# A two-layer decoder's last phase: heads' operands ordered by dimension, and a sync queue gated by the softmax maxima's DMA

## The reference

```
q, k = layernorm over the 8 elements of a head, of x @ Wq.T and x @ Wk.T, times g, plus b
v = x @ Wv.T                                   # 16 heads of 8 elements
x = x + softmax(causal(q @ k.T)) @ v @ Wo.T + bo          # self attention

q = layernorm(x) in 16 heads of 8, k = v = context        # no projections
x = x + softmax(window(q @ k.T / sqrt(8))) @ v @ W_proj.T + b   # |i - j| <= 64

x = x + quantise(layernorm(x)) @ quantised weight.T + bias
```

## Time and profile before

| | |
|---|---|
| median of three runs | 1515.22 us (1513.2 to 1517.85) |
| the profiled execution | 1517.21 us, its span 1514.8 us |
| busy share of the span | PE 87%, DVE 72%, ACT 67%, POOL 42% |
| mean granted TensorE clock | 0.924 of full |
| DMA queue of the sync engine (q1) | 85440 packets, 82.35 MB |
| DMA queue of ScalarE (q10) | 1856 packets, 0.79 MB |

### The profile page before, as it was taken

One profiled execution on the slowest core, in us unless ns is written; L12 is line 12 of the kernel. 1 busy time (PEld: TensorE's weight loads), 2 busy tenths in 40 slices (PEclk: granted clock), 3 DMA queues, 4 the chain that ended last, 5 costly groups with the idle time before them and its releaser, 6 DMA issues.

```text
span 1514.8 us, 42023 instructions
## 1 busy us (share of the span) xinstructions
PE 1325.3 (87%) x14969; PEld 952.1 (63%) x14969; DVE 1089.1 (72%) x2570; ACT 1008.9 (67%) x2781; POOL 632.6 (42%) x842
## 2 busy tenths in 40 slices
PE   4358999999999999999849998888988989888885
PEld 1125666766676666676739997555665656665664
DVE  6998889999999888776663444566765767566664
ACT  2129999999999999999925664354544554545552
POOL 0012324443435243202045452376656564644653
PEclk9999999999999999999969999597878898889995
DMA  6952132424223321020123322223012021110100
GB/s 143 244 126 58 46 75 57 111 52 112 58 72 76 83 56 41 16 78 16 36 86 95 92 80 62 82 37 49 16 39 43 26 44 32 24 37 23 32 18 14
DMA packets 91593, 94.21 MB, mean 62 GB/s; under 512 B 17792, under 2 KB 78848, under 8 KB 86912
## 3 DMA queue, kind: packets, MB, share of 16 engines
q1 hardware_dynamic: 85440, 82.35, 22.5%
q0 software_dynamic: 4096, 8.40, 2.0%
q10 hardware_dynamic: 1856, 0.79, 0.2%
HBM read 64.76 MB, written 17.83 MB: 55 GB/s over the span
## 4 chain that ended last, share of the span: by engine, by line
PE 60%; DVE 14%; ACT 9%; issue 8%; DMA 5%; POOL 3%; SPq 1%; another core or an unknown queue 0%; ACTq 0%; DVEq 0%; POOLq 0%
PE P L794 7%; PE P L956 6%; PE P L2129 6%; PE P L1598 4%; PE P L1631 4%; PE P L812 3%; PE P L938 3%; ACT pr L1017 3%; PE P L915 3%; PE P L2192 3%; PE P L2147 3%; DVE mx L2409 3%; PE P L910 3%; PE P L926 3%; PE P L833 2%
## 5 line engine op out<-in xcount | busy, mean ns | idle before, releaser
L2409 DVE TENSOR_REDUCE mx<-P 128x8 f32<-128x1024 f32 x128 | 156.6, 1224 | 169.7 <-PE P L2129 102.3
L2321 ACT ACTIVATE et<-P 128x1024 f32<-128x1024 f32 x128 | 131.1, 1024 | 191.6 <-PE P L2136 182.8
L1017 ACT ACTIVATE pr<-P,nm 128x256 f32<-128x256 f32 x512 | 238.6, 500 | 5.6 <-DVE nm L1218 5.5
L1218 DVE TENSOR_REDUCE nm<-P 128x4 f32<-128x1024 f32 x128 | 156.2, 1220 | 25.6 <-PE P L794 23.3
L794 PE MATMUL P<-kt_w,qt 64*128 64x256 f32 x1024 | 145.2, 402 | 4.6 <-ACT pr L1017 4.6
L999 ACT COPY ptS<-P 128x512 f32<-128x512 f32 x256 | 138.1, 598 | 8.7 <-PE P L812 8.0
L990 ACT ACTIVATE pr<-pr,ri 128x256 f32<-128x256 f32 x254 | 119.6, 536 | 24.6 <-DVE pr L1191 24.1
L1691 ACT ACTIVATE hT<-P,mixing 128x128 f32<-128x128 f32 x284 | 81.1, 367 | 69.4 <-PE P L1598 63.8
L702 POOL TENSOR_TENSOR kv_qk<-kv_qk,mixing 128x512 f32<-128x512 f32 x48 | 61.0, 1270 | 151.4 <-DVE pr L1191 151.4
L696 POOL TENSOR_TENSOR kv_qk<-kv_qk,r_w 128x512 f32<-128x512 f32 x48 | 61.0, 1270 | 145.5 <-DVE pr L1191 100.1
L1017 ACT ACTIVATION_READ_ACCUMULATOR pr<-P,nm 128x1 f32 x512 | 118.5, 231 | 0.0
(11 more groups left out here) (334 smaller groups left out, 3665.6 us busy)
## 6 DMA issues: line engine op xcount, KB each, us to landing
kv_qk<-scr_v SPq DMA_DIRECT2D x16, 1024.0 KB, 8.0
r_w<-scr_r SPq DMA_DIRECT2D x16, 1024.0 KB, 10.9
xt<-scr_xs SPq DMA_DIRECT2D x71, 64.0 KB
scr_ys<-yt SPq DMA_DIRECT2D x71, 64.0 KB, 1.5
x<-in_x SPq DMA_DIRECT2D x8, 256.0 KB, 10.9
scr_v<-mixing SPq DMA_DIRECT2D x8, 256.0 KB, 2.5
scr_r<-mixing SPq DMA_DIRECT2D x8, 256.0 KB, 2.0
xb<-in_x SPq DMA_DIRECT2D x8, 256.0 KB, 3.4
```

What stands on the lines that cost most here:

```text
L1017: e = nc.scalar.activation(pr[:, s % 3, h * KEYS:(h + 1) * KEYS], scores(s)[:, h // 2, (h % 2) * KEYS:(h % 2 + 1) * KEYS], ACT.Exp, bias=n ...
L1218: nc.vector.tensor_reduce(nm[:, s % 3, 0:4].rearrange("p (a h) -> p a h", a=2), scores(s).rearrange("p a (h k) -> p a h k", k=KEYS), AX.X, ...
L2321: nc.scalar.activation(et[:, u % 4, :, :, :], scoresT, ACT.Exp).then_inc(S["h_exp"], 1)
L2409: nc.vector.tensor_reduce(mx[:, n % 2, 8 * r:8 * r + 8].rearrange("p (k a) -> p k a", k=2), scores, AX.X, ALU.max, negate=True).then_inc(S ...
```

## The change

1. **Packed order.** The 128 partitions of `packed` and `packedE` are now (element c, j, a) in place of (j, element, a): element c of all 16 heads stands on partitions 16c to 16c+15. Everything that writes or reads the packed order follows: the permutation of the weights, the layout of `gbs` (four DMAs to 128 partitions in place of 16 to 32), the sum over a head's elements and its scaling on VectorE, and ScalarE's write of `xnE`.
2. **Spreads.** `spread_heads` issues eight DMAs, one for each element c, from 16 partitions to the four partitions c, c+32, c+64, c+96, in place of four DMAs from 32 partitions to eight neighbouring ones. Both move the same bytes.
3. **Slots.** The self spreads have slots of their own (`spread0` one slot after `kt`, `spread1` two after `qt`; other offsets for groups 1 to 3), and the 16 key DMAs of a local group go four at a time in slots -9, -7, -5 and -3 (`keys0` to `keys3`) in place of all at -10.
4. **Gates.** `turned_maxima(s)` counts the maxima's DMAs issued by slot `s`. The sync engine waits until all of these have landed ahead of a self spread (from group 2 on), a local spread, a load, a group of key DMAs and a store.

```
@@ tables (SELF; the other tables likewise)
-        "kt": -12, "qt": -11}
+        "kt": -12, "qt": -11, "spread0": -11, "spread1": -9}
@@ LOCAL
-LOCAL = {"load": -10, "e_stat0": -8, ...
+LOCAL = {"load": -10, **{f"keys{b}": 2 * b - 9 for b in range(GS)}, "e_stat0": -8, ...
@@ first phase
-  for j, m in ((i // 4, i % 4) for i in range(16)):
-      sp.dma_start(gbs[32 * j:32 * j + 32, m:m + 1], bcast(d["gbqk"][m, 0:DH], 1, 4))
+  for m in range(4):
+      sp.dma_start(gbs[:, m:m + 1], bcast(d["gbqk"][m, 0:DH], 1, H))
@@ vector: weights, scaling, sum over a head
-  spread = wqk[...].rearrange("p (j c a) -> p a j c", j=4, c=DH)
+  spread = wqk[...].rearrange("p (c j a) -> p a j c", j=4, c=DH)
-  x = qkv[...].rearrange("p b (j c a) -> p (b j) c a", c=DH, a=4)
+  x = qkv[...].rearrange("p b (k c h) -> p (b k) c h", c=DH, h=H)
-  nc.vector.tensor_reduce(v3, qkq[...].rearrange("p b (j c a) -> p (b j) a c", c=DH, a=4), AX.X, ALU.add)
+  nc.vector.tensor_reduce(v3, qkq[...].rearrange("p b (k c h) -> p (b k) h c", c=DH, h=H), AX.X, ALU.add)
@@ spread_heads
-  for j in range(4):
-      sp.dma_start(dst[32 * j:32 * j + DH, :, cols], src[32 * j:32 * j + 32, cols])
+  for c in range(DH):
+      sp.dma_start(dst[c:128:32, :, cols], src[H * c:H * c + H, cols])
@@ third phase
+  def turned_maxima(s):
+      return 16 * min(s // 2, UNITS_H // 2)
@@ sync_program
-  g = self_at(s, name)
+  g = self_at(s, f"spread{k}")
...
+  if g >= 2:
+      sp.wait_ge(S["in_q"], turned_maxima(s))
   spread_heads(sp, dst[g % 2], packed[:, k, :], slice(0, N), f"in_sd{g % 2}")
...
+  sp.wait_ge(S["in_q"], turned_maxima(s))
   spread_heads(sp, qTe, packedE, slice(b * T, (b + 1) * T), "in_se")
...
+  sp.wait_ge(S["in_q"], turned_maxima(s))
   sp.dma_start(home(g), xres[rows(g)].rearrange("b t c -> t b c"))
...
+  if s >= 2:
+      sp.wait_ge(S["in_q"], turned_maxima(s))
   sp.dma_start(ctk[:, g % 2, :, :], d["ctx"][rows(g)].rearrange("b t c -> t b c"))
-  for j in range(4):
-      for b in range(GS):
+  for b in range(GS):
+      g = local_at(s, f"keys{b}")
+      if g is not None:
+          if s >= 2:
+              sp.wait_ge(S["in_q"], turned_maxima(s))
+          for j in range(4):
                   sp.dma_start(kTe[32 * j:32 * j + DH, g % 2, :, b * T:(b + 1) * T], ...)
...
   sp.wait_ge(S["h7_read"], filled("fmm", g))
+  sp.wait_ge(S["in_q"], turned_maxima(s))
   sp.dma_start(d["out"][rows(g)].rearrange("b t c -> t b c"), home(g))
```

More of the change, by code:

```diff
@@ L107 @@
         "guess": 17, "inv0": 18, "inv1": 19, "norm0": 20, "norm1": 20,
-        "kt": 21, "qt": 22},
+        "kt": 21, "qt": 22, "spread0": 21, "spread1": 23},
     3: {**{f"gather{k}": 9 + k for k in range(2 * GS)},
@@ L130 @@
 FRONT_SPREAD = 69
-LOCAL = {"load": -10, "e_stat0": -8, "e_stat1": -4, "e_stat2": -2, "e_stat3": 0, "e_nm0": -7, "e_nm1": -3, "e_nm2": -1,
+LOCAL = {"load": -10, **{f"keys{b}": 2 * b - 9 for b in range(GS)}, "e_stat0": -8, "e_stat1": -4, "e_stat2": -2, "e_stat3": 0, "e_nm0": -7, "e_nm1": -3, "e_nm2": -1,
          "e_nm3": 1, "e0": -6, "e1": -2, "e2": 0, "e3": 4, "v0": -3, "v1": -1, "v2": 1, "v3": 3,
@@ L1110, in setup @@
                 for k in range(2):
-                    spread = wqk[:, k * 128:(k + 1) * 128].rearrange("p (j c a) -> p a j c", j=4, c=DH)
+                    spread = wqk[:, k * 128:(k + 1) * 128].rearrange("p (c j a) -> p a j c", j=4, c=DH)
                     nc.vector.tensor_tensor(spread, wD[:, k * 128:(k + 1) * 128].rearrange("p (a j c) -> p a j c", j=4, c=DH),
@@ L1441, in normed @@
         def normed(qkv, g, k, y3):
-            x = qkv[:, g % 2, 2 * k:2 * k + 2, :].rearrange("p b (j c a) -> p (b j) c a", c=DH, a=4)
-            nc.vector.tensor_tensor(x, x, bcast(y3[:, 16 * k:16 * k + 16, :], 2, DH), ALU.mult).then_inc(S["d_qkn"], 1)
+            x = qkv[:, g % 2, 2 * k:2 * k + 2, :].rearrange("p b (k c h) -> p (b k) c h", c=DH, h=H)
+            nc.vector.tensor_tensor(x, x, bcast(y3[:, 4 * k:4 * k + 4, :], 2, DH), ALU.mult).then_inc(S["d_qkn"], 1)
         def spread_heads(sp, dst, src, cols, sem):
-            for j in range(4):
-                sp.dma_start(dst[32 * j:32 * j + DH, :, cols], src[32 * j:32 * j + 32, cols]).then_inc(S[sem], 16)
+            for c in range(DH):
+                sp.dma_start(dst[c:128:32, :, cols], src[H * c:H * c + H, cols]).then_inc(S[sem], 16)
         def second_phase(homes):
@@ L1779, in vector_program @@
                 v, y, u = hn3[:, 0, :], hn3[:, 1, :], hn3[:, 2, :]
-                v3, y3 = [a.rearrange("p (m a) -> p m a", a=4) for a in (v, y)]
+                v3, y3 = [a.rearrange("p (m h) -> p m h", h=H) for a in (v, y)]
                 def sums(g, b):
@@ L1810, in front @@
                         dve.wait_ge(S["d_sq"], 1)
-                        link(dve, nc.vector.tensor_reduce(v3, qkq[:, :, :].rearrange("p b (j c a) -> p (b j) a c", c=DH, a=4), AX.X, ALU.add))
+                        link(dve, nc.vector.tensor_reduce(v3, qkq[:, :, :].rearrange("p b (k c h) -> p (b k) h c", c=DH, h=H), AX.X, ALU.add))
                         link(dve, nc.vector.tensor_scalar(v, v, 1.0 / DH, LN_EPS, ALU.mult, ALU.add))
@@ L1937, in self_spread @@
             def self_spread(g):
-                return 16 * 8 * (g // 2 + 1)
+                return 16 * 2 * DH * (g // 2 + 1)
+            def turned_maxima(s):
+                return 16 * min(s // 2, UNITS_H // 2)
             def local_spread(g, b):
-                return 16 * 4 * (GS * g + b + 1)
+                return 16 * DH * (GS * g + b + 1)
             def head_at(r, t, j):
@@ L1951, in copied @@
             def copied(eng):
-                eng.wait_ge(S["in_g"], 16 * 17)
+                eng.wait_ge(S["in_g"], 16 * 5)
             def sync_program(sp):
```

10 lines of the change are left out of this document (5 added, 5 removed), and 2 rows, old and new, of the table SELF_BY_SLOT.

## The result

The changed kernel takes 1504.31 us (median of 20 runs, 1492.6 to 1516.78), the kernel before beside it 1513.22 us (20 runs, 1504.71 to 1531.69): ratio 0.9932, 95% interval 0.9906 to 0.9958. In a later session, beside 29 runs of before, it gave 0.9943 (0.9914 to 0.9973), 1505.29 against 1515.68 us. So it is faster by 9 to 10 us; 17 were forecast. Each ratio in this document is taken over the runs that lie no more than 1.5% above the fastest of the same kernel, while a time in us is the median of all.

The account below looks back on a forecast made before the run. The third phase's chain was taken as mostly TensorE, which waited 18.6 us for the maxima's DMA behind a spread backlog. Terms -14.1 + 3.3 - 8 + 0.5 = -18.3 us, from 1517.21 us, gave 1498 us; range 1480 to 1520.

Parts of the forecast that it names:

- Maxima's waits: Third phase: TensorE's 18.6 us of waits for the turned maxima's DMA fall to 4.5, saving 14.1 us; bounds 9 and 18.6.
- Gates and order on the sync queue: Sync queue: the maxima's DMA of a pass then meets neither a 256 KB load nor two spreads at once; no separate size.
- Local spreads: Local groups 1 to 5: the fourth spread lands 1.4 to 2.0 us later, costing +3.3 us; bounds 0 and 10.
- Self spreads' landing: Self groups 1 and 2: the landing stays within half a microsecond, counted 0; bounds -1 and +3.
- The clock: TensorE's clock, lower after long waits, partly recovers once those waits go: -8 us; bounds 0 and -17.
- End of the second phase: Stores behind the second spread go out 3 us later and GpSimd's gather waits for them: +0.5 us; bounds 0 and +5.
- Layout: VectorE's sum over a head, scale, ScalarE's write and first-phase weight DMAs cost nothing more: 0; bounds +-1 for eight sums.
- the first: Rival: four DMA engines halve the spread's rate, 7.2 us a spread instead of 3.6; 1524 us, chance 0.09.
- The second: Rival: the new form costs 0.67 us or more to issue, so spreads land late; 1519 us, chance 0.10.
- The third: Rival: VectorE, which caught up during the waits, is late instead and the time returns there; 1513 us, chance 0.09.
- The fourth: Rival: all waits and the whole clock come back; 1483 us, chance 0.15.

## Why the prediction was right, and where it wasn't

The time came out 6 us above the forecast, inside the range, and with the sign forecast. By its steps:

- **Maxima's waits, -14.1 us**: 18.6 to 4.6 us, and 4.9 in the second profile. Right, in size and in reason: no backlog, spread issue 0.52 us (0.54 forecast), maxima's DMA under 3 us in the chain but for one piece of 3.40. The four waits at groups 4 to 7, put at 1 us each, are 1.2, 1.6, 0.5 and 0.3 us.
- **Gates and order on the sync queue**: the prediction laid part of this on the gates. This step was wrong: alone they give 0.9999. It also let the slots' part and the form's stand side by side; either one alone gives all of it.
- **Local spreads, +3.3 us**: 0.4 to 5.1 us, +4.7. The right mechanism, too small: five waits as foreseen, the tightest 2.5 us (1.8 forecast). The forecast's own pieces, two of 1.4 and three of 0.2 us, come to 3.4. A spread lands 2.1 us later (6.3 us against 4.2), since the last issue goes out 2.2 us later and the credit of up to 0.6 us for its quicker landing came to 0.1.
- **Self spreads' landing, 0**: group 1 waits 2.2 us (2.5 before); its last DMA lands 2.5 us after its issue, where it took 5.5 us. Group 2 waited 1.0 or 6.2 us in two executions of one kernel, and before with gates 3.3 against 1.1 without; the bound of +3 was too narrow for a single profile.
- **The clock, -8 us**: the failed term. The prediction put five low pieces, 34 us, down to the long waits and took half of what they cost. In the trace of before the low pieces that follow such a wait (1160 to 1170, 1225 to 1235, 1295 to 1310 and 1365 to 1370 us) are four and come to 27 us of the 132; the rest lie elsewhere. The medians of the clock are 0.924 before and 0.9255 after, in the session that timed both: 1.5 to 2 us. Most of the low clock is there without those waits: from 960 us to the end of the run the profile of before has a clock of 0.84, the two of the changed kernel 0.85. One profile can't carry this term, for the stretch from 980 us that gave the 132 us has 88 us at the lower level in the changed kernel's first profile, 102 in its second, and 114 (980 to 1360) with the gates alone, where all long waits stand. Why the clock varies between runs and variants stays open. This term is 6 us of the 7 to 8 by which the saving fell short.
- **End of the second phase, +0.5 us**: GpSimd waits 9.7 us for the stores against 8.4. Its gather comes 1.0 us earlier than before (935.03 us, 936.01 before), but the work ahead of it was 2.2 us earlier in this profile, so 1.2 us are lost. Within the term's bounds.
- **Layout, 0**: the sum over a head takes 1.90 us against 2.00, 0.1 us less each, eight times. Right for the sum. The scaling behind it (L1444) takes 1.07 us on the mean against 0.94, 16 times, 2 us of VectorE in all; the prediction didn't look at it, and no run shows what of it reaches the time.

With the measured sizes -14.0 + 4.7 + 1.2 - 2 come to -10 us, against the medians' -9 to -10. That the fit is so close is partly luck: in the second profile the wait for group 2's spread alone would take 5 us off the saving.

Of the rivals, the first falls: the DMAs of four destination partitions 32 apart were handed over every 0.56 us, 58 GB/s, above the 50 GB/s below which it was to decide, and between two of them the DMA engines stood still. Its premise holds so far as the small packets are four a DMA, 28 for seven; the rate didn't suffer. By "SBUF — State Buffer" of the Trainium skill, section on the DMA port swizzle, both forms reach two ports; the trace agrees so far as that the new one isn't slower. The second, a late sync queue, is there in kind: 5.1 us of local waits, but the issue got cheaper, not dearer. The third, time that comes back on VectorE, has little for it: DMA waits fell by 9.7 us net in the first profile and by 4.2 in the second, and 8.2 us arrived at an equal clock. So the waits of a single profile account for the time only to within some 5 us. The fourth, 1483 us with the whole clock back, falls with the clock term.

## What to carry to other kernels

A small DMA on another queue can wait several microseconds for a pile of transfers that was handed over just before it; look there, and part the pile in time, in size or by form, since here one of these was enough and form and slots together brought nothing more that could be measured. When a transfer is cut in more pieces, its last landing moves by the extra issues: move its deadline with it, here by one slot, probably worth as much as half the change (4.4 us at an equal clock). And where a kernel's time follows the granted clock from run to run, compare at one clock before a saving is put down to it.

## What the runs showed of the hardware that I had not expected

- An issue's time followed the shape and not the size: a spread DMA onto eight neighbouring partitions took 0.67 us at 64, 32 and 16 KB alike, one onto four partitions 32 apart 0.52 us.
- In runs of one and the same kernel the granted clock varied from 0.914 to 0.935 and the time with it, by 20 us, twice the gain of the change.
- A wait of one profiled execution (group 2's spread) was 1.0 us in one and 6.2 us in the next of the same kernel.
